# A sine-attention and routed-expert block on one core: routed rows grouped by three instead of by two

## The reference, cut to what matters

```
x: (8, 512, 128)                         # 8 rows of 512 tokens, width 128, fp32
x = x + attention(layernorm(x))          # 16 heads of 8; sin(30 * q.k / sqrt 8) in place of softmax
h = layernorm(x)
out = shared(h)                          # silu(h Wg) * (h Wu), then Wd; hidden width 256
probs = sigmoid(h @ Wr.T + rb)           # 8 routed experts
scores, idx = top_k(probs, 2)            # each token takes 2 of the 8
for e in range(8):
    out = out + cw[..., e] * expert_e(h) # cw is zero unless e was taken
x = x + out
```

## Time and profile before

| | |
|---|---|
| median of 3 runs | 538.08 us (536.28 to 540.9) |
| profiled execution | 533.96 us |
| its span, first to last instruction | 532.1 us |
| mean granted TensorE clock | 0.946 of full |
| busy: PE, ACT, DVE, POOL | 447.7, 331.6, 297.6, 259.1 us |
| instructions | 13798 |

### The profile page before, as it was taken

The page is one execution under the profiler, slowest core; times in us unless marked ns, Lnnn a source line. Parts: engine busy times, 40 slices in busy tenths (PEclk is TensorE's granted clock), DMA queues, the critical chain, the costliest instruction groups (busy, mean ns, idle before and its releaser), DMA issues.

```text
span 532.1 us, 13798 instructions
## 1 busy us (share of the span) xinstructions
PE 447.7 (84%) x4616; PEld 238.8 (45%) x4616; DVE 297.6 (56%) x1040; ACT 331.6 (62%) x455; POOL 259.1 (49%) x317
## 2 busy tenths in 40 slices
PE   3289999998986999899975999999977888978871
PEld 1121233324323554455432445444433778966860
DVE  5614363345441646486642756554536698858972
ACT  2189989888975887787773667887754223321320
POOL 5611311201771332248727723268378855698582
PEclk9699999999997999999997899999988989988995
DMA  3789579274033935641357346611123222222111
GB/s 75 219 224 263 126 224 283 47 207 92 31 119 82 189 86 141 139 108 56 105 138 185 87 125 110 166 46 55 36 66 93 77 67 71 68 76 80 52 32 49
DMA packets 87314, 59.84 MB, mean 112 GB/s; under 512 B 30672, under 2 KB 81232, under 8 KB 87248
## 3 DMA queue, kind: packets, MB, share of 16 engines
q1 hardware_dynamic: 80976, 49.58, 37.1%
q0 software_dynamic: 3584, 7.35, 4.9%
q10 hardware_dynamic: 2688, 2.03, 1.3%
HBM read 24.45 MB, written 28.97 MB: 100 GB/s over the span
## 4 chain that ended last, share of the span: by engine, by line
PE 39%; POOL 22%; issue 14%; DVE 9%; DMA 7%; ACT 6%; SPq 1%; ACTq 1%; POOLq 0%; DVEq 0%
PE o_ps L577 10%; POOL x_sorted L1227 8%; PE score L564 7%; POOL hid_lo L1219 6%; POOL y_back L1238 6%; ACT attn L769 4%; PE g_ps L670 3%; PE g_ps L672 2%; PE g_ps L671 2%; DVE hid L1049 2%; DVE x_all L1086 2%; PE d_ps L686 2%; POOL rstd L1206 1%; SPq L441 1%; ACT gate L790 1%
## 5 line engine op out<-in xcount | busy, mean ns | idle before, releaser
L769 ACT ACTIVATE attn<-score 128x1024 f32<-128x1024 f32 x256 | 255.9, 1027 | 66.0 <-PE score L564 63.0
L1219 POOL TENSOR_TENSOR hid_lo<-hid,hid_hi 128x256 f16<-128x256 f32 x148 | 102.4, 692 | 160.1 <-DVE hid_hi L1054 158.8
L577 PE MATMUL o_ps<-attn,vals 128*32 128x512 f32 x1024 | 139.9, 619 | 0.9 <-ACT o_t L776 0.7
L564 PE MATMUL score<-queries,keys 64*128 64x512 f16 x512 | 99.3, 394 | 16.0 <-DMA queries<-q_four 9.5
L564 PEld LDWEIGHTS score<-queries,keys 64*128 64x128 f16 x512 | 24.0, 93 | 134.7 <-issue 74.6
L1049 DVE SCALAR_TENSOR_TENSOR hid<-g_ps,gate 128x256 f32<-128x256 f32 x103 | 43.6, 423 | 71.9 <-ACT gate L790 70.3
L790 ACT ACTIVATE gate<-g_ps 128x256 f32<-128x256 f32 x103 | 39.7, 385 | 57.0 <-PE g_ps L672 47.7
L686 PE MATMUL d_ps<-w_all,hid_hi 128*128 (+1 forms) x200 | 40.9, 227 | 20.8 <-POOL hid_lo L1219 9.7
L670 PE MATMUL g_ps<-xt,w_all 128*128 128x128 f16 x256 | 51.0, 228 | 5.3 <-DMA xt<-x_sorted 5.0
L1054 DVE CAST hid_hi<-hid 128x256 f16<-128x256 f32 x148 | 49.4, 334 | 5.1
L672 PE MATMUL g_ps<-xt,w_all 128*128 128x128 f16 x256 | 51.3, 229 | 0.0
(11 more groups left out here) (181 smaller groups left out, 917.1 us busy)
## 6 DMA issues: line engine op xcount, KB each, us to landing
y_sorted<-y_sb SPq DMA_DIRECT2D x84, 64.0 KB, 1.8
k_four<-k_minus SPq DMA_DIRECT2D x16, 256.0 KB
q_four<-q_parts SPq DMA_DIRECT2D x14, 256.0 KB, 2.5
queries<-q_four SPq DMA_DIRECT2D x14, 256.0 KB
keys<-k_four SPq DMA_DIRECT2D x14, 256.0 KB
x_sorted<-zeros SPq DMA_DIRECT2D x2, 1472.0 KB, 10.8
queries<-q_three SPq DMA_DIRECT2D x14, 192.0 KB
keys<-k_three SPq DMA_DIRECT2D x14, 192.0 KB
```

The lines of the kernel that those rows point to most:

```text
L564: mm = pe.matmul(score[h][:, i, :], keys[b % 2][rows, 2 * j + h, kt * P:(kt + 1) * P], queries[b % 2][rows, 2 * j + h, :], start=True, sto ...
L577: mm = pe.matmul(o_ps[32 * i:32 * i + 32, :], vals[b % 2][:, kt, h:h + 32], attn[k % RING][:, i, :], start=(k == 0), stop=(k == UNITS - 1))
L769: act.activation(attn[k % RING][:, 2 * (u % 2):2 * (u % 2) + 2, :], score[u % 2][:, :, :], ACT.Sin, scale=SIN_SCALE).then_inc(sined, 1)
L1219: pool.tensor_tensor(hid_lo[i % HB][:, :], hid[i % HR][:, :], hid_hi[i % HB][:, :], ALU.subtract).then_inc(hid_lo_ready, 1)
```

## The change

The rows 0 to 6 go in three groups instead of four, and the semaphores that count gathers follow the longest group:

```diff
-ROUTE_GROUPS = [(0, 1), (2, 3), (4, 5), (6,)]
+ROUTE_GROUPS = [(0, 1, 2), (3, 4, 5), (6,)]
...
-        cleared, scattered, gathered = sem("cleared"), sem("scattered"), sems("gathered", 2)
+        cleared, scattered, gathered = sem("cleared"), sem("scattered"), sems("gathered", max(len(rows) for rows in ROUTE_GROUPS))
```

## The result

| | before | changed |
|---|---|---|
| median | 538.62 us (534.97 to 542.75, 20 runs) | 540.21 us (538.38 to 541.65, 20 runs) |
| profiled execution | 533.96 us | 538.61 us |
| span | 532.1 us | 536.7 us |

The ratio is 1.004, with a 95% interval of 1.0021 to 1.0059: slower by 1.6 us, within the 1% that I had called no change. The two profiled executions differ by 4.65 us; the forecast was 4.9. But the median of the changed kernel was forecast at 543.0 and is 540.21.

A forecast was written before the change was run, and what follows sets the result against it. Sines on ScalarE pace 4-tile rows, TensorE 16-tile rows, GpSimd the tail's tiles beside gathers. 4.0 - 13.4 - 9.4 - 6.9 + 30.6 = +4.9 us: 543.0 against a median of 538.1, range 530 to 551.

The forecast's parts named there:

- the clear: Larger clears delay row 2's keys, and its sines never win it back: +4.0 us, ends 0 and 5.
- the tail: From hid_lo of slot 256 to the end: 147.8 us instead of 117.2, +30.6, with more tiles and gathers.
- rows 3 and 4: Attention rows: 88.4 us against 101.8, -13.4; the stall for the first sparse tile moves to row 4, equally long.
- row 5: Attention row with 16 tiles, no scatter or gather, no GpSimd wait for a store: 52.8 us instead of 62.2, -9.4.
- row 6: Attention row with the same tiles and its five scatters starting as before: stays at 52.5 us.
- row 7 to slot 256: GpSimd's scatters, gathers and hid_lo set the time until slot 256's hid_lo: 54.0 us instead of 60.9, -6.9.
- I carry the difference, not the level, over to their median: The +4.9 us against the profiled execution is added to the timed runs' median of 538.1, giving 543.0.
- slots 256 to 275: Start of the tail: 19 steps with a scatter or gather each at 1.86 us, plus waits: 37.9 us, before 31.7.
- The rest of the tail: After slot 275: 9.9 us with combine, 29.5 without gathers, 43.5 with the second group's gathers, 27.0 for the end.
- Faster: Rival, chance 0.17: GpSimd's lag absorbed, TensorE sets row 7 and the tail's start; sum -6.1, 532 us.
- No change: Rival, chance 0.20: the pieces cancel, the tail's start takes 31.7 us as now; sum -1.3, 537 us.
- Slower still: Rival, chance 0.18: gathers lengthen beside VectorE's work, 0.1 us for each of 48, +4.8: 548 us.

The follow-up runs named there:

- e10: The changed kernel, unchanged, timed again in the third session on chip 4: 561.35 us, ratio 1.026 to the kernel before.
- e9: The kernel before, unchanged, one execution in the third session on chip 4: 541.18 us, span 539.3 us.
- e1: The kernel before, unchanged, one more execution in the first session: 536.4 us, span 534.6 us.
- e17: The changed kernel with clears ten slots later and the first group's 24 scatters at two of every three slots: 538.01 us, ratio 0.9886.
- e2: The kernel before with sorted buffers and clears of 31 tiles, the change's larger clear alone: 543.23 us, ratio 1.0092.
- e3: The changed kernel with both clears ten slots later, behind the load of row 2's keys: 532.29 us, ratio 0.9883.
- e4: The kernel before with the first loads of groups two and three two slots later, behind the previous group's last store: 522.33 us, ratio 0.9689.
- e11: The kernel before with the later first loads of groups two and three and the clears at slots 58 and 60: 539.09 us, ratio 0.9835.
- e8: The changed kernel with hid_lo of the tail's tiles beside a gather on VectorE instead of GpSimd: 592.13 us, ratio 1.0899.

## Why the prediction was wrong

The sum held, and what failed was the step from it to the medians. That the sum came so close, +4.6 for +4.9, is partly luck: the clear and the tail were forecast 4.9 us too low, the rows between them 5.5 too high, and the errors cancel.

| stage | forecast, changed less before | measured | with pauses: e10 less e9 |
|---|---|---|---|
| row 0 | 0 | 0.0 | +2.1 |
| clear, row 1 | +4.0 | +5.9 | +3.1 |
| rows 3 and 4 | -13.4 | -15.2 | -3.1 |
| row 5 | -9.4 | -10.3 | -10.3 |
| row 6 | 0 | -1.0 | -1.4 |
| row 7 to slot 256 | -6.9 | -8.7 | -3.9 |
| tail | +30.6 | +33.6 | +33.0 |
| span | +4.9 | +4.6 | +19.4 |

What the stages' sums lack to the span is rounding and the 0.2 us by which row 0 starts later.

- **The step that failed** is "I carry the difference, not the level, over to their median". Before's profiled execution is 4.7 us under its own median of 20 runs, the changed kernel's 1.6 under its own. Their difference of 3.1 us is nearly all of the miss of 3.3 (+4.9 forecast, +1.6 measured): +4.65 between the executions is +1.6 between the medians. The level of one execution doesn't carry over, and neither does the difference of two. It isn't shown what makes before's profiled executions the fast ones. All three of them were under the median of their session (by 4.7, 2.0 and 6.9 us), the three of the unchanged changed kernel that have a median by 1.6, 0.75 and -1.7. A second one of before (e1) is 2.5 us longer than the first, 1.9 of it in row 0, and against it the changed kernel would have been at +2.1.
- **A price was left out.** In two further sessions the same kernel was at 1.026 and 1.029, and in a single execution 3% above before. The condition lengthens rows 4 and 7, where the change has made runs of 24 scatters out of runs of 16. e17 shows that other slots for the scatters lower the price; it doesn't separate the length of the run from the rest. I had asked whether transfers lengthen beside other engines (they don't: the median is 0.96 us in e10 too), and not whether other engines pause beside transfers.
- **The clear** was read rightly as a delay of the keys, and came out at +5.9, above my upper end of 5. e2 has it alone at about 5 and e3 takes it away. The 4.7 at the clears' own mean (4.5, with all sizes in the same unit) was nearer than the 3.1 at the rate of one window, but neither counts what then delays the load: the traffic stays at over 300 GB/s until 92 us instead of 88, and SP's wait for `k_four` behind it is 1.4 longer. The Trainium skill (DMA: Bandwidth & Descriptors, section Bandwidth) would have given 3.1 as well, by its figure for a 1 MB transfer, which it measured on a load into SBUF; the delay in the runs was 5 to 5.9.
- **Rows 3 and 4**: the stall moved as I said. Row 4 is 1.8 shorter than forecast, since the first sparse silu comes 6.3 us after the last scatter and not 8.3. **Row 5**: the wait for the store is gone, and e4 shows the same wait's worth on the kernel before, 6.7 us in that row. Rows 5 and 6 are both 1.0 under the 16-tile rows of before; why isn't known.
- **Row 7** took 52.2 where I had 54.0, and **slots 256 to 275** 41.6 where I had 37.9: together 93.8 against 91.9. My rate of 1.86 us held once the queue was full ((426.48 - 411.33) / 8 = 1.89 between gathers), but in the first nine slots GpSimd waits for `hid_hi` four times for 1.1 to 1.5 us, 5.6 in the whole stretch, for which I had 1.5:

```profile
POOL hid_lo L1219 <- DVE hid_hi L1054: 5.6, 7, 1.5
```

- **The rest of the tail** came out step by step: 10.3, 28.9, 43.1 and 27.0 us where I had 9.9, 29.5, 43.5 and 27.0.
- **The rivals.** "Faster" needed slot 275 under 81 us after row 7's start and got 93.8. "No change" by its mechanism, 31.7 us for the start of the tail, was wrong (41.6), though the median lies near its number; right number, wrong reason. "Slower still" by longer gathers is refuted: they take 0.96 to 1.07 us in the stretch with tiles, as before. The rate of 1.375 us a slot in "Faster" stands in no row; the 1.36 of rows 3 and 4 gives the same. The rule of the Trainium skill (SBUF — State Buffer, section SBUF: two separate sides) that I had weighed is about VectorE holding up GpSimd's transfers. What the runs show is not that: the transfers keep their pace while TensorE's updates come late and ScalarE and VectorE wait.

**Open.** What condition brings the pauses (chip 4 showed them in one session and not in the next), and what makes TensorE's updates late beside the transfers. The recording itself is a rival that no run excludes: every execution has a recorded span, and the traces of the same sessions hold fewer semaphore records. In e11's row 5 late updates cover 7.3 us, enough for the 5.7 that it is longer than in e4, but no run takes them away there.

## What to carry over

Take the sum of a change from a trace, but take its sign from medians of both kernels on several chips: here one kernel was at 1.004, 1.026 and 1.029 of the kernel before. Look at what else stands in a queue before you regroup the work: the wait that the grouping removed could be had for one line (0.9689), and the transfer that it lengthened stood ahead of a load that everything waited for. Don't let an engine that issues transfers run through 24 of them while others need its results: with two tiles moved out of the row as well, two of three slots were worth 1% without pauses, and the pauses cost rows 4 and 5 3 us less.

## What the runs showed beside it

- **Pauses beside runs of indirect transfers.** In three of five sessions ScalarE, TensorE and VectorE stood idle together for 1.3 to 5.2 us at a time in row 4 while GpSimd issued its transfers (e8 has ten spells of 1.2 to 4.8 us in its rows and tail), and updates of TensorE's semaphores came up to 9.8 us late (19.6 in e8). In the two other sessions and in its first profile the same kernel ran through the same row with at most one such spell, of 2.1 us, at its end, and no update came 1 us late. The traces of the sessions with pauses hold fewer semaphore records for the same instructions (about 7,500 to 7,850 against 8,950 to 9,660), so some weren't recorded; whether that has the same cause is not known.
- **The kernel before pays as well, but less:** its median was 538.4 to 539.5 in sessions without pauses and 542.2 to 548.1 in those with them, where its rows 3, 5 and 7 show 26 late updates (e9).
- **An indirect transfer is short everywhere:** its median on GpSimd is 0.95 to 0.98 us with tiles beside it, alone, or in a pause, the longest of all takes 1.48; the pace of a run is 1.25 to 1.27 us.
- **A clear of 2 x 1984 KB** holds SP's queue for 8.11 us (6.09 for both of 1472 KB), and what stands behind it waits longer than that: the row's own stores of k land late, and the load of the keys, which needs them, was issued at 95.49 instead of 89.56.
